# A first batch normalised, turned and partly projected ahead of the barrier between two phases

## The reference

```python
x = x + _L0_attn_a_ref(_layernorm(x, axis=-1), ...)
x = x + _L0_ffn_ref(_layernorm(x, axis=-1), ...)     # 8 experts, the best 2 of each token
x = x + _L0_attn_b_ref(_layernorm(x, axis=-1), ...)  # the state-space block
x = x + _L0_ffn_ref(_layernorm(x, axis=-1), ...)
```

```python
xn = _ln(x, norm_g, norm_b)          # x is already a layernorm
concept_preserved = (xn @ Wconcept.T + bconcept) * sigmoid(xn @ Wcg.T + bcg)
forget_gates = sigmoid(xn @ Wfg.T + bfg)
sp = xn @ Wsp.T
u = complex(sp[..., :nf], sp[..., nf:]) * forget_gates
...                                   # a long convolution over the tokens by FFT, a gate, an MLP
```

## Time and profile before

| | us |
|---|---|
| median of 3 timed executions | 600.17 |
| lowest and highest of them | 600.0, 608.57 |
| the profiled execution's own time | 605.27 |
| its span, first to last instruction | 603.5 |
| TensorE busy | 505.4 (84%) |
| VectorE busy | 383.2 (63%) |
| ScalarE busy | 239.7 (40%) |
| GpSimd busy | 318.9 (53%) |

### The profile page before, as it was taken

One profiled execution on the slowest core, in us unless ns is written; L12 is line 12 of the kernel. 1 busy time (PEld: TensorE's weight loads), 2 busy tenths in 40 slices (PEclk: granted clock), 3 DMA queues, 4 the chain that ended last, 5 costly groups with the idle time before them and its releaser, 6 DMA issues. The chain is left out here.

```text
span 603.5 us, 12179 instructions
## 1 busy us (share of the span) xinstructions
PE 505.4 (84%) x3512; PEld 351.3 (58%) x3513; DVE 383.2 (63%) x1284; ACT 239.7 (40%) x489; POOL 318.9 (53%) x372
## 2 busy tenths in 40 slices
PE   4989999989989977866997597899987848869991
PEld 2454455635635436766997243644666547869991
DVE  4898888776787865741546656641595776633454
ACT  1345577755656833322444442101022413323440
POOL 1504556797366574574545576046151777763552
PEclk9999999988989987997999598799997988998997
DMA  6353233142232114443446100000000113222254
GB/s 188 92 169 86 76 112 124 61 130 76 80 106 67 42 41 108 119 118 85 113 111 169 42 0 0 1 0 1 1 0 1 36 41 85 85 77 62 71 157 122
DMA packets 46535, 46.10 MB, mean 76 GB/s; under 512 B 8677, under 2 KB 39968, under 8 KB 46336
## 3 DMA queue, kind: packets, MB, share of 16 engines
q1 hardware_dynamic: 38490, 33.60, 20.1%
q0 software_dynamic: 4544, 9.35, 4.6%
q10 hardware_dynamic: 3446, 2.47, 1.3%
HBM read 31.68 MB, written 15.12 MB: 78 GB/s over the span
## 5 line engine op out<-in xcount | busy, mean ns | idle before, releaser
L1314 ACT ACTIVATE store<-ps 128x512 f32<-128x512 f32 x160 | 91.4, 595 | 57.4 <-PE ps L881 57.1
L1098 DVE TENSOR_REDUCE at_mx<-ps 128x1 f32<-128x512 f32 (+1 forms) x128 | 73.6, 615 | 21.7 <-PE ps L868 21.6
L473 POOL DMA_INDIRECT expert_rows<-r_rows,r_sloti x64 | 62.7, 980 | 33.7 <-DVE r_sloti L311 17.0
L866 PE MATMUL ps<-at_hats 72*128 72x512 bf16 (+3 forms) x256 | 69.5, 308 | 3.4 <-DVE at_mx L1095 1.7
L881 PE MATMUL ps<-at_hats 74*128 74x512 bf16 (+3 forms) x256 | 61.7, 305 | 0.8 <-DMA at_hats<-at_mT 0.8
L659 POOL DMA_INDIRECT expert_results<-at_vall x39 | 38.3, 982 | 44.2 <-DVE at_vall L601 35.3
L1402 POOL TENSOR_SCALAR_AFFINE_SELECT store<-store 128x512 f32<-128x512 f32 x64 | 39.5, 644 | 40.5 <-ACT store L1314 40.5
L659 POOL DMA_INDIRECT expert_results<-store x39 | 38.1, 977 | 36.0 <-DVE store L601 31.3
L898 PE MATMUL ps<-store,at_vext 128*32 128x128 f32 (+3 forms) x512 | 51.1, 477 | 1.3 <-ACT at_oT_more L1284 1.3
L868 PE MATMUL ps<-c_mask_q_bf,c_ident_bf 128*128 128x128 bf16 x256 | 50.4, 222 | 0.0
L633 PE MATMUL ps<-at_vall,at_hats 128*128 128x128 f32 x312 | 44.5, 289 | 4.4 <-issue 2.0
(11 more groups left out here) (328 smaller groups left out, 1046.2 us busy)
## 6 DMA issues: line engine op xcount, KB each, us to landing
at_hats<-parts SPq DMA_DIRECT2D x48, 96.0 KB
at_hats<-parts SPq DMA_DIRECT2D x16, 288.0 KB
moe_w<-moe_w_dram SPq DMA_DIRECT2D x8, 512.0 KB, 4.8
store<-ssm_tables_dram SPq DMA_DIRECT2D x35, 86.0 KB
at_vall<-expert_rows SPq DMA_DIRECT2D x39, 64.5 KB
store<-expert_rows SPq DMA_DIRECT2D x39, 64.5 KB
sm_gates<-expert_results SPq DMA_DIRECT2D x8, 256.0 KB, 4.1
at_hats<-expert_results SPq DMA_DIRECT2D x6, 256.0 KB, 4.2
```

Of the source, the lines that this page charges most:

```text
L473: pool.indirect_dma_start(self.xs_dram[:, :], bass.IndirectOffsetOnAxis(self.sloti[:, n, k:k + 1], 0), self.rows[:, k, n, :], None).then_i ...
L866: pe.matmul(bankA(n)[:, col:col + (t + 1) * P], hatq[0:MROW, slot, h, t * P:(t + 1) * P], hatk[0:MROW, slot, h, 0:(t + 1) * P], start=True ...
L1098: m = dve.tensor_reduce(mx[:, u % 2, t, h:h + 1], bankA(n)[:, 0:(t + 1) * P], AX.X, ALU.max)
L1314: act.activation(pt[:, u % 2, j // 2, S * (j % 2):S * (j % 2 + 1)], bankB(n), ACT.Exp).then_inc(s_e, 1)
```

## The change

A new class, `FirstBatch`, takes batch 0's normalisation, transposes, affine step and the first three of its four projections into the first phase, on the buffers of the router's rows, which are free by then. Its semaphores belong to the whole kernel and are not cleared between the phases, so the second phase goes on counting from them. For batch 1 ScalarE scales the results in the first phase, behind the sines of the rotation table, and VectorE adds them with one instruction for each k. The semaphores of `add_scaled` now count by GT = 4, like those of `add`.

```diff
@@ Results.add_scaled
         if k:
-            dve.wait_ge(self.s_sum, 1)
-        dve.tensor_tensor(xg, xg, self.of(k, g), ALU.add).then_inc((self.s_sum, self.s_out)[k], 1)
+            dve.wait_ge(self.s_sum, GT * (g - self.first + 1))
+        dve.tensor_tensor(xg, xg, self.of(k, g), ALU.add).then_inc((self.s_sum, self.s_out)[k], GT)
@@ attention, TensorE
             over_slot_tiles(pe, lambda i, u: experts.tensor(pe, i, u), begin=8)
+            head.turn(pe)
+            head.project_ahead(pe)
@@ attention, VectorE
             norms.moments(dve, 0)
             expert(NSLOT + 1)
-            results.add(dve, 1, 0)
             expert(NSLOT + 2)
-            results.add(dve, 1, 1)
+            head.normalize(dve)
+            results.add_scaled(dve, 1, 0)
+            results.add_scaled(dve, 1, 1)
             results.settle(dve, 1)
             norms.moments(dve, 1)
             results.combine(dve, 2)
@@ attention, ScalarE
             turns.sines(act)
+            for k in range(2):
+                experts.combined.scale(act, 1, k)
+            act.activation(warm[:, :], c["eps"][:, :], ACT.Sigmoid)
+            head.affine(act)
@@ attention, GpSimd
             for i in range(NSLOT - 2, NSLOT + 4):
+                if i == NSLOT + 3:
+                    norms.inverse_root(pool, 0, 1)
                 expert(i)
-            norms.inverse_root(pool, 0, 1)
@@ new
+class FirstBatch:
...
+        self.xh = room[:, 0:S].rearrange("p (t d) -> p t d", d=D)
+        self.xnT = room[:, S:2 * S]
+        self.bankT = ps[:, 0, :]
+        self.bankS = lambda i: ps[:, 1 + i % 3, 0:TOK]
+        self.bankV = lambda b: ps[:, 4 + b % 2, :]
+
+    def normalize(self, dve):
+        self.norms.rooted(dve, 0, 1)
+        for t in range(TPB):
+            dve.tensor_scalar(self.xh[:, t, :], self.x[:, t, :], self.norms.mv[:, t, 0:1], self.norms.rstd[:, 1, t:t + 1],
+                              ALU.subtract, ALU.mult).then_inc(self.s_xh, 1)
+
+    def turn(self, pe):
+        pe.wait_ge(self.s_xh, TPB)
+        for t in range(TPB):
+            mm = pe.transpose(self.bankT[:, t * P:(t + 1) * P], self.xh[:, t, :], self.c["ident"][:, :])
+        mm.then_inc(self.s_t, 1)
+
+    def affine(self, act):
+        act.wait_ge(self.weights_loaded, 16 * (len(self.w) - 1))
+        act.wait_ge(self.s_t, 1)
+        act.activation(self.xnT, self.bankT, ACT.Identity, bias=self.w["norm_gb"][:, 1:2],
+                       scale=self.w["norm_gb"][:, 0:1]).then_inc(self.s_xc, 1)
+
+    def project(self, pe, xt, i):
...
+    AHEAD = 3
+
+    def project_ahead(self, pe):
+        pe.wait_ge(self.weights_loaded, 16 * (len(self.w) - 1))
+        pe.wait_ge(self.turns.s_made, 1)
+        pe.wait_ge(self.s_xc, 1)
+        for i in range(self.AHEAD):
+            self.project(pe, self.xnT[:, i * P:(i + 1) * P], i)
@@ ssm, VectorE
-            normalize(0)
+            normalize(1)
             norms.moments(dve, 2)
-            normalize(1)
...
+            concept(0)
+            concept(1)
             late.add_scaled(dve, B - 1, 0)
-            concept(0)
             normalize(2)
-            concept(1)
             late.add_scaled(dve, B - 1, 1)
             concept(2)
-            dve.wait_ge(late.s_out, 1)
+            late.settle(dve, B - 1)
             norms.moments(dve, 3)
@@ ssm, ScalarE
-            affine(0)
-            late.scale(act, B - 1, 0)
             gate(0)
-            late.scale(act, B - 1, 1)
             gate(1)
             affine(1)
-            for i in range(2, 6):
+            late.scale(act, B - 1, 0)
+            gate(2)
+            late.scale(act, B - 1, 1)
+            for i in range(3, 6):
                 gate(i)
@@ ssm, TensorE
-            transposed(0)
+            transposed(1)
             for b in range(B):
...
-                for t in range(TPB):
+                for t in range(0 if b else head.AHEAD, TPB):
                     project(b * TPB + t)
-                    if t == 1 and b + 1 < B:
+                    if b and t == 1 and b + 1 < B:
                         transposed(b + 1)
```

More of the change, by code:

```diff
@@ L687, with attention @@
 WIDTH = [S - P * k for k in range(TPB)]
-def attention(nc, ps, x, x_rows, c, consts, att, parts_dram, router, turns, norms, experts, store, load_moe_weights, load_ssm_weights):
+def attention(nc, ps, x, x_rows, c, consts, att, parts_dram, router, turns, norms, experts, head, store, load_moe_weights, load_ssm_weights):
     with ExitStack() as ctx:
@@ L1756, in rooted, with __init__ @@
             engine.wait_ge(self.s_rstd[k], b - self.roots_done[k] + 1)
-def ssm(nc, ps, x, c, w, weights_loaded, tables_loaded, router, turns, norms, experts, out):
+class FirstBatch:
+    def __init__(self, nc, ctx, ps, x, c, w, weights_loaded, turns, norms, room):
+        self.x, self.c, self.w, self.weights_loaded, self.turns, self.norms = x, c, w, weights_loaded, turns, norms
+        self.s_xh, self.s_t, self.s_xc, self.s_ps, self.s_pv = (
+            ctx.enter_context(nc.semaphore(f"tokens_{k}")) for k in ("normalized", "turned", "scaled", "projected", "values"))
+        self.xh = room[:, 0:S].rearrange("p (t d) -> p t d", d=D)
[19 more added lines that the diff above has]
+    def project(self, pe, xt, i):
+        b, t = i // TPB, i % TPB
+        pe.matmul(self.bankS(i), self.c["ones_bf"][0:3, :], self.turns.bias[:, :], start=True, stop=False)
+        pe.matmul(self.bankS(i), xt, self.w["wtok"][:, 0:TOK], start=False, stop=True).then_inc(self.s_ps, 1)
+        mm = pe.matmul(self.bankV(b)[:, t * P:(t + 1) * P], xt, self.w["wtok"][:, TOK:TOK + D], start=True, stop=True)
+        if t == TPB - 1:
+            mm.then_inc(self.s_pv, 1)
+    AHEAD = 3
[5 more added lines that the diff above has]
+            self.project(pe, self.xnT[:, i * P:(i + 1) * P], i)
@@ L1761, in ssm @@
+def ssm(nc, ps, x, c, w, weights_loaded, tables_loaded, router, turns, norms, experts, head, out):
     with ExitStack() as ctx:
@@ L1807, in ssm @@
         s_ch = sem("dve_chain")
-        s_xh = sem("xh")
-        s_t, s_xc = sem("xnT_psum"), sem("xnT_copied")
-        s_ps, s_pv, s_pb = sem("gates_psum"), sem("values_psum"), sem("band_psum")
+        s_xh, s_t, s_xc, s_ps, s_pv = head.s_xh, head.s_t, head.s_xc, head.s_ps, head.s_pv
+        s_pb = sem("band_psum")
         s_sig, s_bsig, s_cp = sem("gates"), sem("band"), sem("concept")
@@ L1820, in ssm @@
         s_o, s_x, s_xs = sem("out_psum"), sem("x"), sem("x_x2")
-        bankT = ps[:, 0, :]
-        bankS = lambda i: ps[:, 1 + i % 3, 0:TOK]
-        bankV = lambda b: ps[:, 4 + b % 2, :]
+        bankT, bankS, bankV = head.bankT, head.bankS, head.bankV
+        xnT_of = lambda b: xnT[:, b % 2, :] if b else head.xnT
         bankB, bankW = ps[:, 6, :], ps[:, 7, :]
@@ L2288, in project @@
                 b, t = i // TPB, i % TPB
-                xt = xnT[:, b % 2, t * P:(t + 1) * P]
+                xt = xnT_of(b)[:, t * P:(t + 1) * P]
                 if t == 0:
@@ L2295, in project @@
                     pe.wait_ge(s_cp, i - 2)
[L2296 to L2300, removed]
+                head.project(pe, xt, i)
             def band(b):
@@ L2307, in band @@
                 h = b % 2
-                pe.matmul(bankB[h * NF:(h + 1) * NF, :], w["wband"][:, :], xnT[:, b % 2, :], start=True, stop=True,
+                pe.matmul(bankB[h * NF:(h + 1) * NF, :], w["wband"][:, :], xnT_of(b), start=True, stop=True,
                           skip_group_check=True).then_inc(s_pb, 1)
@@ L2679, in whole @@
         experts = Experts(ps, x, c, mw, router, xs, ys, s_mw)
+        head = FirstBatch(nc, ctx, ps, x, c, sw, s_sw, turns, norms, router.rows[:, :, :, :].rearrange("p k t o -> p (k t o)"))
         def load_ssm_weights(sp, i):
@@ L2691, in load_ssm_weights @@
             sp.dma_start(sw["tables"][:, at], ssm_w["tables"][:, at]).then_inc(s_tab, 16)
-        attention(nc, ps, x, x_rows, c, consts, att, parts, router, turns, norms, experts, store, load_moe_weights, load_ssm_weights)
-        ssm(nc, ps, x, c, sw, s_sw, s_tab, router, turns, norms, experts, out_rows)
+        attention(nc, ps, x, x_rows, c, consts, att, parts, router, turns, norms, experts, head, store, load_moe_weights, load_ssm_weights)
+        ssm(nc, ps, x, c, sw, s_sw, s_tab, router, turns, norms, experts, head, out_rows)
 def kernel(**inputs):
```

## The result

The changed kernel took **614.92 us** in the median of four executions (613.3 to 620.56), the kernel before 604.37 in four (600.0 to 614.39), three of which are the ones that the forecast was put on. The ratio is 1.0272, 95% interval 1.0189 to 1.0354, for a prediction of 604.9 and a range up to 609.5. Every ratio in this document leaves out executions more than 1.5% above the fastest of their kernel, while medians and means take all. The medians differ by 10.5 us, the means by 10.1. The profiled execution took 613.3.

What follows compares the result with a forecast made beforehand. The phase barrier, then GpSimd's row from the root of batch 3, was taken to bound the kernel. Barrier 8.0 us later, less 3.3 saved behind it, gives +4.7 on 600.2: 604.9 us, range 599.5 to 609.5.

Steps and rivals of the forecast that it cites:

- The seam: Barrier between the two phases: 8.0 us later, 3.3 saved behind it, so GpSimd's root of batch 3 4.7 us later.
- my upper bound: Clock never rises ahead of the barrier, and half a microsecond is lost on ScalarE behind it: +5.9, 606.1 us.
- 343.0: Forecast end of TensorE's three projections ahead of the barrier, making it the last engine, 8.0 us later than VectorE was.
- 344.5: Forecast start of phase two, 1.5 us behind TensorE's end, where it was 336.5 before.
- 9.9: Forecast us from phase two's beginning to GpSimd's root of batch 3, where it was 13.2.
- that half microsecond: Part of the upper bound, behind the barrier: half a microsecond lost where ScalarE alternates scaling and gates.
- ScalarE's strand: Behind the barrier, ScalarE's and VectorE's chain from first root through scaling, gate and add to batch 3's moments: 9.85 us.
- 6.6 us behind the first projection: TensorE ahead of the barrier: clock rises 6.6 us behind the first projection's start, as before, so projections end at 343.0.
- one later stretch: Low clock between 373 and 384, 10.2 us, may vanish or be joined by another: 599.8 to 610.0 us; chance 0.18.
- The barrier that doesn't wait for matmuls: Rival at the barrier: VectorE's 338.4 decides, phase two begins at 339.9; +0.1, 600.3 us; chance 0.08.
- TensorE at 2.4 GHz ahead of the barrier: Rival: the moved projections and transposes keep the full clock; +1.2, 601.4 us; chance 0.07.
- my slower rival: TensorE stays at 1.2 GHz behind the barrier: 604.9 + 1.23 us per projection on the path, up to 616; chance 0.09.

Runs made afterwards that it cites:

- the two larger comparisons: Changed kernel rerun against the kernel before on one chip, +5.0 ± 1.9 us; both kernels with three unread matmuls in TensorE's 2.1 us idle time, 5.6 ± 1.4 us.
- filled_after: Changed kernel plus three unread matmuls in TensorE's 2.1 us idle time at the router's rows; mean 605.4 us, +2.9 ± 1.7 against the kernel before.
- again: The changed kernel, unedited, run again beside the kernel before on the same chip; mean 609.3 us, +5.0 ± 1.9, ratio 1.0041.
- scaled_only: Kernel before with only batch 1's results scaled by ScalarE and added by VectorE in phase one; mean 604.7 us, +0.4 ± 1.6, ratio 1.0023.
- warm_before: Kernel before plus seven unread matmuls behind TensorE's last slot tile; mean 602.3 us, −1.1 ± 1.5 against the kernel before, ratio 0.9999.
- warm_scaled: Kernel before with batch 1's results scaled by ScalarE, plus seven unread matmuls behind TensorE's last slot tile; mean 605.6 us, +2.3 ± 1.8, ratio 1.0022.

## Why the prediction was wrong

The seam was forecast 4.7 us longer, and the two larger comparisons give 5.0 ± 1.9 and 5.6 ± 1.4. The first four executions gave 10.5. So two things are to be told apart: a mechanism that was right with one term of it mis-sized, and a sum that was put on too few executions.

**The seam, right in kind, and as large as my upper bound.** The root of batch 3 is 5.9 later relative to E, for 4.7 forecast and 5.9 given as the bound. TensorE's DRAIN was the last, at 15.2 behind E where 343.0 meant 14.6, and phase two's first instruction stands at 16.8 where 344.5 meant 16.1. From there to the root it took 10.4 and not 9.9. The bound had that half microsecond, but from the wrong place: ScalarE's strand was through 0.9 us early, and it was GpSimd's residual that took 0.53 longer than in the earlier trace rows. What slowed it, no run here tests. VectorE's DRAIN ended at 9.7 for 10.0. Turning back batch 2 is 5.9 later too (380.18 − 331.2 = 48.9, for 371.50 − 328.4 = 43.1): the shift does carry through, as forecast.

**The mis-sized term: the rise of the clock.** I carried over "6.6 us behind the first projection" from one opening. TensorE was dense for 8.1 us at 338.3 to 346.4 and the clock stayed at 0.50, so the 0.65 us that I had taken off for its rise was not there. In `filled_after` it rose inside the third projection, whose last matmuls take 0.39 for the 0.64 at 1.2 GHz (timeline of TensorE, the first projection and that end):

```profile
327.95 0.53 PE L1803 MATMUL ps<-tu_bias,c_ones_bf 3*128 3x449 bf16 x1 [1.02 <-ACT r_rows L1798]
...
335.38 0.39 PE L1805 MATMUL ps<-store,r_rows 128*128 128x128 f32 x2
```

So the same opening has its rise before 7.4 us once and not within 8.1 another time. The Trainium skill (TensorE: Matmul & The Clock Gate, "What's actually happening") says that the array is throttled by default and that sustained activity releases it, with a start that varies between runs. The trace agrees with the direction and with the variation, and the variation is what my sum left out: 8.1 us of dense work did not release it here, and the 33 busy microseconds of `again` above ran at 0.66 in the mean.

**The failed step: the price of the clock elsewhere, and the base.** I added 4.7 to 600.17, the median of three executions, and priced the clock elsewhere at one later stretch and at most 5.1 us. But executions of the unchanged kernel lie between 595.2 and 616.1 (105 of them, mean 603.0, deviation 5.0). The time goes with the clock: each 0.01 of mean granted clock is 4 us, correlation −0.88 over those 105. So the mean of four executions is uncertain by 2.5 us, and a difference of two such means by 3.6; the 10.1 between them is 1.2 times that above the 5.9 of the seam. The base itself was 2.8 below the mean of 105; with that mean and the seam's 5.9 the forecast would have been 608.9. So no further step of the change is needed for the miss. In the profiled execution the part outside the seam is the clock: the low stretch at 32 to 46 puts the first router transposes 3.15 us late (135.46 for 132.31), and 2.8 of it is left at E. For the three executions without a profile this is argued only, from their mean clocks of 0.905, 0.905 and 0.913, for 0.921 in the profiled one. The four are also high for this very program: in `again` 5 of 13 executions took 613.3 us or more, here all four did, and whether that is chance or something of that occasion the runs don't tell.

**The rivals.** The barrier that doesn't wait for matmuls is refuted by 68, 2755 and 8115 ns. The Trainium skill (VectorE: DVE Perf Modes, "The DRAIN you can't avoid") gives the DRAINs of preamble and postamble as about 12 ns, constant. These durations show that this doesn't carry over to a DRAIN at the end of a block, as this rival had it. TensorE at 2.4 GHz ahead of the barrier occurred only in the kernels made for it. The low clock behind the barrier, my slower rival, did occur until 361, and cost nothing on the path: the root of batch 3 followed GpSimd's own row without idle time, and from it to the turning back of batch 2 it is 21.8 us as before. The later stretch moved the other way, −0.8 from the root to the end. VectorE waited 3.2 us for the root, not 2.

**What stays open.** Why the clock stayed up behind the 2.1 us of idle time in `scaled_only` alone, and why it stays low for 3.4 us once and 24 another time, isn't settled; no row tells these apart.

## What to carry to other kernels

Work that is moved ahead of a barrier is free there only if it ends ahead of the engine that was last. Otherwise weigh what it adds to the last arrival (here 8.7) against what it takes off behind (2.8), and cost it at the clock that the moved matmuls will meet after their idle time. Before a difference of a few microseconds is forecast on a median of three, compare the profile's parts ahead of the change with other executions, and give the range what they vary by.

## What the runs showed of the hardware

- The DRAIN that ends a block on TensorE lasts until its matmuls are done: 68 ns, 805 ns, 2.8 us and 8.1 us for nothing under way, part of a tile, one and three projections.
- The granted clock can stay at 1.2 GHz through dense work: 8.1 us ahead of the barrier here, and in `again` from 132 to 156. It fell at 2.1 us of idle time in nine of ten profiles; with work in that gap it didn't in any of four.
- Filling idle time with unread matmuls held the clock in some places and failed in others, with the same matmuls at the same place (`warm_before`, `warm_scaled`).
